# The low half of tile 4's rows ahead of two finishes on VectorE, and the wait for the last landings moved from GpSimd to SyncE

## The reference

```
x = x + tanh(g_xattn) * attention(layernorm(x), ctx, ctx)
xf = layernorm(x)
probs = softmax(xf @ w_router); topk_w, topk_idx = top_k(probs, 2)
h   = gelu(xf @ w1[e] + b1[e])                 # 256 -> 1024, for the two experts of a token
out = sum over the two of topk_w * (h @ w2[e] + b2[e])
x = x + tanh(g_ffn) * out
```

## Time and profile before

| | us |
|---|---|
| median of 3 runs | 714.89 (714.8 to 718.47) |
| the profiled execution, its own time | 716.8 |
| its span, first to last instruction | 715.0 |
| TensorE busy with matmuls | 684.9 |
| VectorE busy | 480.2 |
| ScalarE busy | 339.7 |
| GpSimd busy | 317.5 |

### The profile page before, as it was taken

One profiled execution on the slowest core, in us unless ns is written; L12 is line 12 of the kernel. 1 busy time (PEld: TensorE's weight loads), 2 busy tenths in 40 slices (PEclk: granted clock), 3 DMA queues, 4 the chain that ended last, 5 costly groups with the idle time before them and its releaser, 6 DMA issues.

```text
span 715.0 us, 21473 instructions
## 1 busy us (share of the span) xinstructions
PE 684.9 (96%) x6737; PEld 619.8 (87%) x6738; DVE 480.2 (67%) x1246; ACT 339.7 (48%) x708; POOL 317.5 (44%) x422
## 2 busy tenths in 40 slices
PE   6899999999999998989999999999999999999992
PEld 5799999999999887878998998989989989989882
DVE  6688788887887866775665665655756656656551
ACT  4677767777777754322342332433423423324320
POOL 7323676777765657742332332322323323323323
PEclk9999999999999999999999999999999999999997
DMA  6233444445444543326332333323323323233222
GB/s 194 61 133 116 160 158 156 165 145 180 163 129 155 171 140 113 90 32 169 48 52 52 45 52 53 45 46 58 46 45 46 52 51 45 47 57 45 49 29 29
DMA packets 53086, 64.71 MB, mean 90 GB/s; under 512 B 4577, under 2 KB 48743, under 8 KB 52903
## 3 DMA queue, kind: packets, MB, share of 16 engines
q1 hardware_dynamic: 38415, 44.81, 20.6%
q0 software_dynamic: 14512, 19.14, 16.2%
q10 hardware_dynamic: 104, 0.04, 0.0%
HBM read 38.34 MB, written 25.54 MB: 89 GB/s over the span
## 4 chain that ended last, share of the span: by engine, by line
PE 54%; POOL 4%; issue 3%; DVE 2%; DMA 1%; DVEq 0%; POOLq 0%
PE banks L1504 26%; PE banks L1526 26%; PE banks L1516 2%; POOL routed L735 2%; POOL l_exp L718 1%; DMA out_dram<-prob_t,meta 1%; DVE prob L1131 1%; POOL out_dram L756 0%; DVE prob_t L1149 0%; POOL rstd L691 0%; DVE xn_t L1138 0%; DVE prob_t L1153 0%; DVE v_area L1133 0%; POOL x_res L702 0%; DVEq L590 0%
## 5 line engine op out<-in xcount | busy, mean ns | idle before, releaser
L858 ACT ACTIVATE stage<-banks,bias_t 128x256 f32<-128x256 f32 x312 | 131.0, 471 | 272.6 <-PE banks L1504 271.3
L1504 PE MATMUL banks<-xn_t,w_hi 128*128 128x256 f16 x1248 | 208.3, 274 | 3.6 <-DVE xn_t L1138 3.6
L756 POOL DMA_INDIRECT out_dram<-prob_t,meta x78 | 124.7, 1598 | 191.1 <-DVE prob_t L1153 173.1
L1504 PE MATMUL banks<-xn_t,w_lo 128*128 128x256 f16 x624 | 170.9, 274 | 0.0
L1526 PE MATMUL banks<-w_hi,v_area 128*128 x624 | 170.1, 273 | 0.0
L1526 PE MATMUL banks<-w_lo,prob 128*128 x624 | 170.1, 273 | 0.0
L1526 PE MATMUL banks<-w_hi,prob 128*128 x624 | 170.1, 273 | 0.0
L1504 PEld LDWEIGHTS banks<-xn_t,w_hi 128*128 x1248 | 122.5, 98 | 18.6 <-issue 4.1
L1133 DVE TENSOR_TENSOR v_area<-stage,prob 128x512 f16<-128x512 f32 x156 | 108.4, 695 | 5.4
L1149 DVE SCALAR_TENSOR_TENSOR prob_t<-banks,arena 128x256 f32<-128x256 f32 x78 | 32.9, 422 | 117.0 <-PE banks L1526 115.0
L735 POOL DMA_INDIRECT routed<-row,pos x64 | 71.4, 1116 | 28.2 <-issue 15.7
(11 more groups left out here) (214 smaller groups left out, 980.2 us busy)
## 6 DMA issues: line engine op xcount, KB each, us to landing
stage<-in_L_ffn_w_dram SPq DMA_DIRECT2D x32, 512.0 KB, 4.0
x_row<-routed SPq DMA_DIRECT2D x39, 265.0 KB, 2.8
x_in<-in_x_dram SPq DMA_DIRECT2D x16, 256.0 KB, 3.4
x_res<-in_x_dram SPq DMA_DIRECT2D x16, 256.0 KB, 3.9
out_dram<-x_res SPq DMA_DIRECT2D x16, 256.0 KB, 2.7
routed<-pad_rows SPq DMA_DIRECT2D x9, 265.0 KB
out_dram<-prob_t,meta POOLq DMA_INDIRECT x78, 3.8
routed<-row,pos POOLq DMA_INDIRECT x64, 3.4
```

The source lines that it names most:

```text
L756: pool.indirect_dma_start(out[:, :], bass.IndirectOffsetOnAxis(ap=meta_of(j, pj)[:, b, E:E + 1].bitcast(U32), axis=0), y[:, pj, b], None, ...
L858: ins = act.activation(hid[:, c], H[:, q, c % PER * SLOTS:(c % PER + 1) * SLOTS], ACT.Gelu_apprx_tanh, bias=k.bias_t[:, bass.ds(e * HC + c ...
L1504: mm = pe.matmul(H[:, q, c % PER * SLOTS:(c % PER + 1) * SLOTS], w[:, bass.ds(e, 1), i, c * P:(c + 1) * P].rearrange("p a n -> p (a n)"), ...
```

## The change

VectorE computes the low half of tile 4's rows and splits the hidden values of tile 3 directly behind the final plan, and finishes tiles 1 and 2 (the second and the third) behind that. The list from tile 4's split on is as before. The wait for the last landings goes from the end of GpSimd's list to the end of SyncE's.

```diff
@@ SyncE
                 tile_pipeline(sp, step, EARLY_TILES - 2)
+                for i in range(2):
+                    sp.wait_ge(added[i], 16 * SB * ((MAX_TILES + 1 - i) // 2))
@@ GpSimd
                 tile_pipeline(pool, step, 2)
-                for i in range(2):
-                    pool.wait_ge(added[i], 16 * SB * ((MAX_TILES + 1 - i) // 2))
@@ VectorE
                 dve.tensor_scalar(k.row_of[:, EARLY_TILES:EARLY_TILES + NT], row_f[:], float(E * REGION), None, ALU.min)\
                     .then_inc(plan, 1)
+                low_rows(4)
+                for q in range(HID_BANKS):
+                    split_hidden(3, 1, q)
                 finish_rows(1, 0, 1)
-                tile_pipeline(dve, step, 3)
+                finish_rows(2, 1, 0)
+                tile_pipeline(dve, step, 4)
```

## The result

The changed kernel is slower: 718.88 us as the median of 13 runs (717.66 to 723.2) against 716.18 us for 13 runs of the kernel before (714.79 to 719.12), a ratio of 1.0044 with a 95% interval of 1.0028 to 1.006. By the ratio that is 3.2 us (2.7 between the medians), just inside the 0.5% that I called no change, and 718.88 lies over the top of my range, 718.2. The profiled execution took 717.68 us with a span of 715.9, only 0.9 over the one of before (715.0). The profiled execution of before stood 0.6 us over the median of its kernel, this one stands 1.2 under that of its own. Where these 1.8 us come from is the first question of the experiments.

The account below looks back on a forecast made before the run. TensorE, busy for 96% of the span, was taken as the bound. Tile 7's +2.1 us and the last wait's -2.5 us gave -0.4 on the median of 714.89: 714.5 us, range 711.8 to 718.2.

Parts of the forecast that it names:

- The mechanism at tiles 4 to 7: Tile 4's wait goes; tile 1's later finish delays tile 6's load, and the padding stores delay tile 7's: +2.1 us.
- The tight place at tile 5: VectorE finishes tile 5's low half at about 320, just before TensorE wants it at 320.7.
- Step 1: At tile 7, TensorE's transposes begin at 343.7 and not 341.66, as the stores bind the load: +2.1 us.
- So this place costs 2.94 + (7.08 - 5.24) = 4.78 us: At tile 4's first layer, TensorE's idle time of 2.94 us plus 1.84 us of low clock, both expected to go.
- Step 2: At the end, GpSimd's DRAIN starts at 707.96, takes the same 4.39 us and ends at 712.35: 2.5 us gained.
- The bounds, 0 and 4.4: Lower and upper bound, in us, of the gain from moving the last wait to SyncE, so GpSimd's DRAIN starts earlier.
- a DRAIN that starts near 710: Sign of being right: GpSimd's last DRAIN starts near 710 (707.96 moved by 2.1), before the landing.
- The rule that I weighed from the Trainium skill: DRAINs of a kernel's frame take about 12 ns on all engines; by it the end gains 0 and the sum is +2.1.
- the low clock behind tile 6's wait: Behind a 3.8 us wait for tile 6's rows, TensorE's clock falls again: 1.84 us, hidden before tile 7's rows at 343.7.
- the predicted +2.1 at tile 7: Tile 7's transposes at 343.7 against 341.66, as its load waits for the stores; given as +1.5 to +2.6 us.

Follow-up runs that it names:

- second profile: The kernel before, unchanged, run and profiled once more: ratio 0.9993 to the kernel before, span 713.5 us.
- the stores early: The changed kernel with SyncE's eight padding stores issued directly behind the final plan, ahead of tile 6's load: ratio 1.0032 to the kernel before.
- the trace with the DRAIN in the middle: The kernel before plus a DRAIN between GpSimd's last scatter of routed rows and first transfer into the output: 724.04 us in one execution.

## Why the prediction was wrong

**The mechanism at tiles 4 to 7 was right.** The wait before tile 4's first layer went; the finish of tile 1 moved by 4.5 to 4.9 us (5.1 predicted, 4.6 to 5.6); the load of tile 6 went at 326.03 (326.7), its rows landed at 328.7 (329.7), TensorE waited 3.16 us there (3.8), the load of tile 7 went at 339.99 behind the stores (340.8), and the transposes of tile 7 began at 342.94 (343.7). Turning round the finish and the split, and nothing else, took all of it back. The tight place at tile 5 held too: no wait there. What failed is what these times were counted against, and the price of the DRAIN.

**Step 1 that failed: "TensorE began the transposes of tile 7 at 341.66; now at 343.7", carried to the median by one subtraction.** The 341.66 has the low clock in it that I booked with "So this place costs 2.94 + (7.08 - 5.24) = 4.78 us". I read it, and the wait in front of it, from one profiled execution as properties of the kernel, and took the whole 1.9 us between that execution and the median of three as an offset that the changed kernel would share. The second profile has the same wait without the low clock, at a cost of 3.0 us, and two other traces with VectorE's old order have waits of 2.02 and 0.67 us. What TensorE gives up at tile 7 stands against less than I booked in most traces: against the second profile, the changed kernel's trace is 3.9 us longer in Stage and 1.1 shorter at the end, which makes 2.8 to 2.9 us (2.4 between the spans, as it came to tile 4 0.5 us earlier). That is near the measured 3.2, and far from the 0.9 against the first profile. How often an execution has the low clock stays open, and with it how much of the miss is its.

**How the miss adds up.** The forecast was -0.4 us on the median, and 2.7 came: 3.1 us. The DRAIN makes 1.4 of them (2.5 expected, 1.1 measured). Between the two profiled executions tile 8 came 1.8 us later and not 2.1, which takes 0.3 off. The 1.8 between these executions and their medians is the rest, but for 0.2. Of that, 0.6 is on the side of the kernel before, whose low clock would explain it; the other 1.2, by which the changed kernel's executions are mostly longer than the profiled one, is in no trace here.

**Step 2 that failed: the last wait, "the same 4.39 us from 707.96".** The move gives 1.1 us and not 2.5, in two traces (8.6 to 7.5). I took the DRAIN as a fixed length from the point where GpSimd is free. That held where nothing was still to land; here it ended 3.6 us behind the landing and 5.8 us behind the end of the last transfer's instruction. Where the last 1.4 of these 5.8 come from is open. The bounds, 0 and 4.4, held it. As a sign of being right I had named a DRAIN that starts near 710; its row has it start at 706.8, so the start of a DRAIN's row isn't the time from which its 4.39 us run. The rule that I weighed from the Trainium skill ("VectorE: DVE Perf Modes", section "The DRAIN you can't avoid": about 12 ns for the DRAINs of the preamble and postamble) isn't borne out by any GpSimd DRAIN here: 0.53 us is the shortest. SyncE's 7 ns are near it.

**A term mis-sized: the low clock behind tile 6's wait.** I took 1.84 us, hidden under the stores. Counted the same way, transposes and second layer against 0.44 and 5.24, it was 3.2 us in the changed kernel (1.12 and 7.81) and 3.2 with the stores early, since it lasted twice as long as before. In the changed kernel it filled the time up to tile 7's rows, so the transposes there came by both paths at once. Behind them came 0.3 us more, in which TensorE waited for nothing that the profile shows, and 0.2 in the second layer, so that tile 8 was 1.8 us later than before and not only the 1.3 of tile 7.

**The sum again.** With the second profile as the kernel before, the predicted +2.1 at tile 7 would have read +3.7 (343.7 against 340.04, where that profile has them), and with 1.1 for the end the forecast would have been +2.6, close to the measured 2.7 between the medians. Part of that closeness is luck, as the 1.2 us above are in neither. The range missed by 0.7 us, and for another reason too: it stood on the median of three runs, 714.89, and that of thirteen is 716.18 for the same kernel. A change within 0.5%, to which I gave 0.77, is what came, but barely and with the other sign: its interval reaches 0.6%.

## What to carry to other kernels

When an operation is pulled forward in an engine's list, price what it overtakes by the longest chain that hangs on that, not by the engine's idle time: here a finish of 2 us behind a split of 4.25 was the first link of landings, a copy and a load that TensorE needed two tiles later. A low clock in a profile, and a wait in which two engines race, belong to that execution until a second profile shows them again; ask for one before booking them as a gain. If a block ends with a DRAIN on GpSimd behind many indirect transfers, one more DRAIN where GpSimd idles anyway is worth trying: a line gave 4 us here. Put where GpSimd has work waiting, it held that up for 6 us in the one execution tried.

## What the hardware showed that I had not expected

- GpSimd's DRAIN takes 4.39 us behind 142 indirect transfers, 4.08 behind 136, 4.05 behind 78 and 0.53 behind 6, on an idle engine and with all of them landed.
- The same idle time of 2.9 us left TensorE's clock at 2.4 GHz in two traces (2.85 and 2.88 us, the second that of the wait part alone) and was followed by 1.2 GHz in one (2.94); so was one of 2.58 us in the trace with the DRAIN in the middle. With idle times of 3.16 to 3.91 us the clock fell each time, before the wait was over, for 6.8 us in two traces and 3.4 in one (3.27).
- 265 KB stores from SyncE lengthened the landing of GpSimd's 128-row accumulating transfers from 3.8 and 4.0 us to 4.8 and 5.3; in the kernel before, those beside the stores took 4.6 and 4.9.
